# A four-stage fp32 block on one core: tokens kept feature-major in a rotated basis

## The reference, cut to what matters

```python
x = x + attention(ln(x, 1e-6))          # over the 16 values of n, for each (a, b); 8 heads of 16
t = t + top2_of_8_experts(ln(t, 1e-5))  # token-wise: router 64 -> 8, experts 64 -> 64
x = x + gated_scan(ln(x, 1e-6))         # expand 64 -> 128, scan over a (s = 0.9 s + 0.1 x), sigmoid, contract
t = t + experts_pick_tokens(ln(t, 1e-5))# softmax over the 4096 tokens of an n, top 8 for each of 32 experts
```

## Time and profile before

| | |
|---|---|
| median of 3 runs | 3138.21 us (3133.75 to 3139.93) |
| span of the profiled execution | 3121.5 us; about 17 us lie around it |
| busy: TensorE, VectorE, GpSimd, ScalarE | 2647.5, 2551.6, 2161.0, 2005.1 us |
| mean granted TensorE clock | 0.839 |
| loop | from 38 us to about 2888 us |
| pooling and experts; adding | to about 3034 us; to the end |

### The profile page before, as it was taken

The page is one execution under the profiler, slowest core; times in us unless marked ns, Lnnn a source line. Parts: engine busy times, 40 slices in busy tenths (PEclk is TensorE's granted clock), DMA queues, the critical chain, the costliest instruction groups (busy, mean ns, idle before and its releaser), DMA issues. The chain is left out here.

```text
span 3121.5 us, 108500 instructions
## 1 busy us (share of the span) xinstructions
PE 2647.5 (85%) x37071; PEld 1969.9 (63%) x37071; DVE 2551.6 (82%) x9002; ACT 2005.1 (64%) x3590; POOL 2161.0 (69%) x2963
## 2 busy tenths in 40 slices
PE   2898898888888888898898898888988988896697
PEld 2666666666666656666666666666666666664586
DVE  2788889888888898888888888888889888885604
ACT  2666767766676676776776766677667676762600
POOL 2677777877777777777787877778777777863000
PEclk9788988887888888888887987889889788885858
DMA  0011101111011010110101111011010010101828
GB/s 17 9 20 18 19 17 19 19 18 19 17 19 18 18 19 17 19 19 18 19 17 18 19 18 19 17 19 19 18 19 18 17 19 18 19 15 19 269 96 337
DMA packets 263153, 106.67 MB, mean 34 GB/s; under 512 B 250257, under 2 KB 254900, under 8 KB 258997
## 3 DMA queue, kind: packets, MB, share of 16 engines
q1 hardware_dynamic: 260933, 93.16, 12.9%
q10 hardware_dynamic: 2160, 12.68, 1.0%
HBM read 55.31 MB, written 50.33 MB: 34 GB/s over the span
## 5 line engine op out<-in xcount | busy, mean ns | idle before, releaser
L472 ACT ACTIVATE kT<-s_bank,b_k,block_of 128x512 f32<-128x512 f32 x1024 | 748.8, 771 | 3.6 <-PE s_bank L609 0.3
L640 PE MATMUL s_bank<-kT,qT 128*32 128x128 f32 x8192 | 396.1, 372 | 187.3 <-issue 187.3
L640 PEld LDWEIGHTS s_bank<-kT,qT 128*32 128x32 f32 x8192 | 349.5, 152 | 226.8 <-issue 224.7
L489 ACT ACTIVATE qT<-shared,b_qkg 128x256 f32<-128x256 f32 x256 | 107.5, 471 | 412.0 <-PE shared L609 412.0
L811 DVE TENSOR_REDUCE mixed<-yg 128x256 f32<-128x2048 f32 x128 | 288.5, 2254 | 0.2
L687 PEld LDWEIGHTS o_bank<-w_o,ogT 128*128 128x128 f32 x2048 | 247.9, 193 | 23.7 <-DVE ogT L839 14.8
L414 POOL TENSOR_TENSOR probs<-weights,own_den 128x1024 f32<-128x1024 f32 x128 | 252.7, 1975 | 1.8 <-DVE own_den L857 1.8
L687 PE MATMUL o_bank<-w_o,ogT 128*128 128x64 f32 x2048 | 246.9, 274 | 4.3 <-DVE ogT L839 3.9
L387 POOL TENSOR_TENSOR split_ffn<-norm_ffn,split_ffn 128x256 fp32r<-128x256 f32 x128 | 93.6, 731 | 215.1 <-ACT split_ffn L464 215.1
L658 PEld LDWEIGHTS o_bank<-probsT,v_sb 32*32 32x32 f32 x16384 | 170.2, 107 | 63.7 <-issue 58.1
L658 PE MATMUL o_bank<-probsT,v_sb 32*32 32x64 f32 x16384 | 196.5, 234 | 1.5 <-DVE yg L932 1.5
(11 more groups left out here) (204 smaller groups left out, 7648.6 us busy)
## 6 DMA issues: line engine op xcount, KB each, us to landing
x_in<-in_x SPq DMA_DIRECT2D x1024, 16.0 KB, 1.7
x_scratch<-x SPq DMA_DIRECT2D x1024, 16.0 KB, 1.4
normalized_x_scratch<-norm_pick SPq DMA_DIRECT2D x1024, 16.0 KB, 1.5
xa<-normalized_x_scratch SPq DMA_DIRECT2D x16, 1024.0 KB, 8.1
xb<-x_scratch ACTq DMA_DIRECT2D x8, 1024.0 KB, 10.3
out_x<-xa SPq DMA_DIRECT2D x16, 512.0 KB, 5.3
out_x<-xb SPq DMA_DIRECT2D x16, 512.0 KB, 6.9
xa<-x_scratch SPq DMA_DIRECT2D x4, 1024.0 KB, 6.5
```

The source lines that it names most:

```text
L472: ins = s.activation(kT[:, h, :], bk("k")[:], ACT.Identity, bias=b_k[:, h:h + 1], scale=block_of[:, h:h + 1])
L640: ins = t_.matmul(s_bank[g * 32:(g + 1) * 32, 0, t * P:(t + 1) * P], qT[z][:, c, tok:tok + 32], kT[:, :, tok + c * N:tok + (c + 1) * N], s ...
```

## The change

The loop is written anew; the two blocks behind it change in a few places.

A slot now holds two columns `b` by 16 rows `a` by 16 `n`, again 512 tokens. They are loaded as 128 rows (8 rows `a`, 16 `n`) of two columns of 64 features, transposed once by TensorE, multiplied by a 128 x 128 matrix `T2` (for each column an orthogonal matrix whose first feature is the mean times 8), and stay in this form, 128 partitions (two columns of 64 rotated features) by 256 tokens, until the third stage's result is turned back (`out_of_basis`). In this basis a mean is one feature; weights have its row at zero, so no mean is subtracted. Variances are a square (GpSimd or ScalarE) and a matmul with `ones2`, which leaves them as 128 tokens by 4. Eps is added on VectorE, the power taken on GpSimd. To bring them to the feature-major form the reciprocal deviations are stored to a DRAM scratch tensor (`rstd_store_*`) and read back, each value repeated over 64 partitions (`rstd_spread_*`), by SP. GpSimd multiplies.

Projections are fp32 matmuls with 64-row operands, one for each column, at row positions 0 and 64. The keys have four masks in place of eight, two scores matmuls of 64 rows in place of one of 128. For the experts, the gates (not the outputs) are spread over partitions by a matmul (`gates_spread`), multiplied with the normalized tokens (copied by four SBUF to SBUF transfers, `spread_tokens`; row 0 stays one and carries the bias), and one accumulating group of matmuls yields the mixed result. The scan covers 16 rows at a time and carries its state in column 0. All lags and orders differ, up to 11 slots; the loop body holds four slots. The normalized third result is stored no more: the pooling block reads `x3`, gathers the reciprocal deviations, multiplies them into the transposed picks on VectorE and subtracts the mean with one matmul.

```diff
-LAG = {"att_t": 1, "k": 1, "q": 1, "gate": 1, "v": 1, "scores": 2, ...
-PEELED = 5
+FILLS = [("expand", 8), ("gates_spread", 6), ("project_gv", 2), ("x_transpose", 1), ("project_qk", 2), ("contract", 9), ("experts", 6), ("into_basis", 1), ("attend", 3), ("variance_att", 1), ("variance_conv", 6),
+         ("scores", 2), ("att_out", 3), ("route", 4), ("gates_transpose", 5), ("variance_pick", 9), ("pick", 11), ("variance_ffn", 3), ("out_of_basis", 9)]
+PEELED = 4
...
+    def slots_of(ap):
+        return ap.rearrange("n (q u p) (w h) d -> u q w p n (h d)", q=4, u=2, h=2)
...
+    r_dram = nc.dram_tensor("rstd_scratch", [4, PAIRS, 4, 4, P], F32).ap()
...
+            @block.sync   (order in a slot: spread att, store conv, store ffn, spread conv, spread ffn,
+                           x3_store, spread_tokens, x_load, store pick, spread pick, store att)
+                    if runs(i, q, LAG["rstd_spread_att"]):
+                        z = turn(q, LAG["rstd_spread_att"])
+                        waits(sp, arrived(s_rstd_stored[0], 2, 16, i, q, LAG["rstd_spread_att"]),
+                              done(s_normalized[0], i, q, LAG["rstd_spread_att"], NB["rb"]))
+                        src = r_v[0, pair_of(i, q, LAG["rstd_spread_att"]), z].rearrange("(h u) t -> h (u t)", h=2)
+                        sp.dma_start(rb[0][z % NB["rb"]][:],
+                                     src.unsqueeze(1).broadcast_to([2, D, 2 * P])).then_inc(s_rstd_spread[0][z % NB["rb"]], 16)
+                    if runs(i, q, LAG["rstd_store_conv"]):
+                        z = turn(q, LAG["rstd_store_conv"])
+                        after(sp, s_rstd_done[2], i, q, LAG["rstd_store_conv"])
+                        sp.dma_start(r_v[2, pair_of(i, q, LAG["rstd_store_conv"]), z].rearrange("x t -> t x"),
+                                     rstd[2][z % NB["rstd"]][:]).then_inc(s_rstd_stored[2][z % 2], 16)
...
+                        for k in range(2):
+                            for h in range(2):
+                                sp.dma_start(xdup[z % NB["xdup"]][k * D + 1:(k + 1) * D, h * 256:(h + 1) * 256],
+                                             norm[1][z % NB["z1"]][h * D + 1:(h + 1) * D]).then_inc(s_tokens_spread[z % NB["xdup"]], 16)
...
+                        for u in range(2):
+                            sp.dma_start(x_in[z % NB["x_in"]][:, u],
+                                         x_v[u, z, pair_of(i, q, LAG["x_load"])]).then_inc(s_x_loaded[z % NB["x_in"]], 16)
...
+            @block.gpsimd (first in a slot)
+                        landed(pool, s_rstd_spread[0], NB["rb"], 16, i, q, LAG["normalize_att"])
+                        g.tensor_tensor(norm[0][z % NB["z0"]][:], xr[z % NB["xr"]][:], rb[0][z % NB["rb"]][:], ALU.mult).then_inc(s_normalized[0], 1)
...
+            @block.scalar
+                        for m in (0, 1):
+                            ins = s.activation(keys[z % NB["keys"]][:, m, :].rearrange("p (h t) -> p h t", h=2), two("project_qk")[:, :, 256:512],
+                                               ACT.Identity, bias=b_k[:, m:m + 1], scale=head_mask[:, m:m + 1])
...
+            @block.tensor
+                        for m in range(4):
+                            for h in range(2):
+                                ins = t_.matmul(quad("gates_spread")[:, m, h * 256:(h + 1) * 256], pick_pair[:, h, m * P:(m + 1) * P], gatesT[z % NB["gatesT"]][:])
...
+                            for h in range(2):
+                                ins = t_.matmul(bk("experts")[h * D:(h + 1) * D, 0:256], w_e2[:, m, :], scaled[z % NB["scaled"]][:, m, h * 256:(h + 1) * 256],
+                                                start=(m == 0), stop=(m == 3), tile_position=(0, h * D))
...
+                        for u in range(2):
+                            ins = t_.matmul(bk("variance_att")[:, 0:4].rearrange("p (h u) -> p u h", h=2)[:, u], sq[0][z % NB["sq"]][:, u * P:(u + 1) * P], ones2[:])
...
+            # the pooling block
+                    for q in range(4):
+                        for w in range(2):
+                            for h in range(2):
+                                sp.dma_start(r_rows[q * 32 + w:(q + 1) * 32:2, h], r_from[q, w, h]).then_inc(s_r, 16)
...
-                            s.copy(wT[:, 4 * u:4 * u + 4, :].rearrange("p t m -> p (t m)"), banks[u % 2]).then_inc(s_wt_cp, 1)
...
+                            v.tensor_tensor(wT[:, 4 * u:4 * u + 4, :].rearrange("p t (j e) -> p t j e", j=4),
+                                            banks[u % 2].rearrange("p (t j e) -> p t j e", t=4, j=4),
+                                            r_tok[:, 4 * u:4 * u + 4, 4 * gr:4 * gr + 4].unsqueeze(3).broadcast_to([P, 4, 4, EP]),
+                                            ALU.mult).then_inc(s_wt_cp, 1)
...
+                    dve.wait_ge(s_r, 256)
                     best(0)
```

## The result

The changed kernel takes 5231.1 us (median of 4 runs, 5228.1 to 5239.3), the kernel before 3136.0 (median of 4; the table above has three of them): 1.669 times as long, 95% interval 1.665 to 1.673. The profiled execution has a span of 5226.4 us. The forecast was 3026, at most 3430, so the time lies far outside the range and on the other side.

The account below looks back on a forecast made before the run. It took the two DMA engines running the spreads as the bound: 16.5 us of packets plus 3.6 us idle make a 20.1 us slot; 128 slots plus 453 us outside give 3026 us, range 2540 to 3430.

Parts of the forecast that it names:

- What bounds the kernel before; the engines' work: Old slot bound by TensorE's order, tied to ScalarE's keys; new work per slot: VectorE 13.3 us, ScalarE 10.7, GpSimd 12.6, TensorE 13.4.
- Half of the time it runs at half its clock: In the kernel before, TensorE inside a slot is hardly idle but runs half of the time at clock 0.50.
- TensorE's halves: The two halves of projections, experts and output projection run side by side, 4.3 us instead of 8.6.
- Compute allows 15 to 18 us: Engine work and the dependency chain of 14.9 us across a slot would permit a slot of 15 to 18 us.
- The spreads on two engines, 48 ns a packet: Each rstd spread runs on 2 DMA engines, 48 ns per 1 KB packet; four spreads take 12.3 us a slot.
- a slower pair: Rival: the two DMA engines need more per 1 KB packet; 58 ns gives 3360 us, 80 ns 4080; chance 0.27.
- sixteen engines: Rival: spreads run on sixteen DMA engines, so compute decides; slot 16.5 us, 2565 us in all; chance 0.20.
- 0.2 us until the store has landed: SP's idle wait for an rstd store before issuing the spread, three times a slot, taken as 0.2 us each.
- The term of three turnarounds: Three times a slot the DMA pair idles, 0.2 us for the store and 1.0 to the spread's first packet: 3.6 us.
- the pair of DMA engines: The two DMA engines that run the spreads, each carrying 16.5 us a slot of spreads, copies, token transfers and small stores.
- the clock rival: Rival: TensorE, granted clock 0.5 for half of the slot, needs some 19 us; slot 21.5 us, 3205 us; chance 0.13.
- Setup and tail: Outside the slots: 373 us before, plus 5 setup, 30 filling and 45 tail (31 of it VectorE's late first maximum), 453.

Follow-up runs that it names:

- the run with far stores and no wait: Changed kernel with rstd values stored 64 bytes apart, spreads and the tail's gather reading input x, no wait for the stores; 2942 us, ratio 0.933.
- the best version: Changed kernel, three norms' rstd stored in 16-byte pieces and spread as 2 KB rows, the pick's via TensorE and ScalarE, tail gathers first; 3020 us, ratio 0.967.

## Why the prediction was wrong, step by step

**What bounds the kernel before; the engines' work.** Right in the main. "Half of the time it runs at half its clock" holds for the slot of the earlier trace rows only: a mean of 0.86 leaves some 28% of the time for the lower of two levels. Per slot VectorE has 322.65 / 26.75 = 12.1 us (forecast 13.3), ScalarE 9.4 (10.7), GpSimd 12.8 (12.6). TensorE's halves do overlap for a good part: eight instructions of 256 columns in 1.14 us and sixteen in 1.95 at the full clock are 0.12 to 0.14 us each, against 0.22 one behind the other. TensorE was still too short: 21.8 us at a clock of 0.66 here, and 17.7 at 0.89 in the run with far stores and no wait (901 / 51), where the forecast had 13.4 at the full clock. "Compute allows 15 to 18 us" was not seen either: that run's slot is 19.6. Whether TensorE alone sets those 19.6 was not taken apart, since its spreads still run on two DMA engines. It did not matter for the miss; it is one reason why mended stores only come back to the time before, the other being the 2.6 us of round trips.

**The spreads on two engines, 48 ns a packet.** Right: 130 packets, 47 ns. The landing was not: beside slow stores a spread was used 5.6 us after its issue at best and up to 11 (2029.91 to 2040.99), instead of 3.5 to 4.5; with the stores in 512-byte rows it took 4.6 to 4.8. One step of it was short, the time to the first packet: the 1 KB packets of the spread issued at 2505.33 begin at about 2507.2, 1.9 us later, where the forecast had 1.0. The rivals of a slower pair and of sixteen engines both fall. Giving the spreads sixteen engines saved nothing as long as the stores were slow; with mended stores it was never changed alone. The Trainium skill's rule on the outermost dimension ("DMA: Bandwidth & Descriptors", "Rules for kernel authors") agrees with the 128 + 2 packets. The stores' own packets were mis-added: 4 x 32 at 8 ns are 1.0 us, not 1.3.

**The step that failed: "0.2 us until the store has landed".** It took the 1.4 us of the earlier trace rows, which are stores of long rows, for a store of 512 values of 4 bytes side by side, and gave this landing no upper bound at all, though I bounded the packets of the same store from both sides. Measured: 9.2 us to landing, three waits of 7.8 in a slot in place of 0.2 each. The term of three turnarounds, 3.6 us, is 26.0 in the slot shown. With the stores in 512-byte rows, the waits and spreads as they were, the slot is 21.7 and the time 3141: this term is the miss. That these stores also hold up the transfers beside them (4311 us without any wait) was in no rival.

The form of the sum was wrong as well. It took the pair of DMA engines as busy for 16.5 us and idle in the turnarounds; with 26.0 for them it would give 42.5 us, and the slot is 37.4. The spreads' packets move while SP waits for a store, and what fills the rest of the slot is SP's issuing: 10.9 us for the other twelve transfers, where the forecast had 8 for all sixteen and called it no bound.

**What of the sum held with mended stores.** The rest of 20.1 against 21.7 is 1.6 us: the round trip waits 2.5 us twice, and the bare floor is 19.6, not 16.5. Neither number was mine; that 20.1 lay close to 21.7 is luck, two errors that met: a compute floor too low and a pair of DMA engines that was taken as busy all through the slot.

**TensorE's clock.** A mean of 0.66 looks like the clock rival, but it goes with the waits: with shorter waits it is 0.83 (512-byte rows) and 0.89 (far stores, no wait) with the same matmuls. It is not the cause of the slot; whether it lengthens it at all, as that rival said, no run shows, since SP's gaps and issues are already the whole slot.

**Setup and tail.** Right: 444 us outside the slots against 453. VectorE's first maximum of the tail begins 33 us after the tail's first issue of SP (forecast 31; in the kernel before the two began together), and the tail is 270 us from there on, 37 longer than before (forecast 45):

```profile
4989.63 4.43 DVE L1189 MAX8 best<-picks 128x8 f32<-128x4096 f32 x1 [64.35 <-DMA r_tok<-rstd_scratch]
```

```profile
4956.57 0.37 SPq L1067 DMA_DIRECT2D w<-in_L_ffn_weight  x1
```

**Range and chances.** The range was built from the price of the spread and left the store's landing as a point. A single term of unknown size that stands three times on the path of every slot is worth 128 x 3 = 384 us for each microsecond; with 0.3 us more the forecast would no longer have been faster ((3138 - 3026) / 384). That multiplication would have shown where to look.

## What to carry to other kernels

A store is priced by its shape in memory before its bytes: give the landing of a transfer that something waits for a bound of its own, from a row of the same shape, and multiply it by how often it stands on the path. Values that lie across partitions should leave in pieces of 16 bytes or more, or in rows; and where a wait looks like the cause, take it away once without taking away the transfer, as this shows whether the transfer also blocks its queue. When such a mend comes back only to the old time, look at the next bound (here TensorE, busy for 85 to 90% of a slot, and the time of an issue) before adding instructions to either.

## What the runs showed of the hardware

- 512 writes of 4 bytes in one transfer to device memory land in 9.2 us when they are adjacent, 5.6 with 8 bytes from one to the next, 3.3 with 16 or 64; 256 adjacent ones need 9.0. 128 pieces of 16 bytes need 3.0 (1.8 in the best version).
- Such a store, adjacent 4-byte writes, showed no packet and no busy DMA engine for its last 3.7 us, and beside such stores a spread of 1 KB rows was used up to 11.5 us after its issue (4.6 to 4.8 beside 512-byte rows).
- An issue on SyncE's queue took 0.25 to 0.33 us for a store of four 512-byte rows, 0.37 to 0.41 for one of 128 rows of four values, 0.5 to 0.6 for a spread, and 0.54 for each of four stores of 128-byte rows, which started 0.74 us apart.
- GpSimd's power takes 0.16 us for each element of a partition (41.1 us for 256), 1.0 us for four.
- GpSimd's multiplication of 256 columns took 0.85 us with one operand read at a stride of four, 0.72 without, in two of the three norms; the third took 1.17 and 1.20.
